# Two attention layers and an expert layer on one core: the batch loop turned by half, the next batch's projections between this batch's last pair and its outputs

## What is computed

```python
# layer 1: self-attention over x, 16 heads of 32
attn = softmax(inner @ outer.T / sqrt(32)) * aperture[..., :, None] * expression[..., None, :]
attn = attn / (attn.sum(-1) + 1e-8);  converged = attn @ v
x1 = layernorm(x + rotate_and_scale(converged) @ Wout)
# layer 2: attention of x1 over ctx, with a mask of 1024 x 1024 for each batch, 16 heads of 32
x2 = layernorm(x1 + softmax(mask(q @ k.T / sqrt(32))) @ v @ Wo + bo)
# layer 3: routed expert attention over x2
```

## Time and profile before

| | us |
|---|---|
| three runs | 4908.39, 4911.23 (median), 4921.20 |
| the profiled execution | 4916.44 |
| its span, from the first to the last instruction | 4914.7 |
| TensorE busy | 4307.2 (88%) |
| VectorE busy | 2653.4 (54%) |
| ScalarE busy | 1568.2 (32%) |
| GpSimd busy | 902.7 (18%) |
| layer 1: first exp of batch 0, last pv of batch 3 | 136.7, 1784.7 |
| layer 2: first exp of batch 0, last pv of batch 3 | 1986.5, 3785.7 |
| last transpose of layer 2 begins | 3834.2 |

### The profile page before, as it was taken

How to read it: one execution, slowest core, us unless ns; L and a number is a source line. 1 busy time by engine, 2 the same in 40 slices (tenths; PEclk the granted TensorE clock), 3 DMA queues, 4 the chain that set the end, 5 groups by cost and what they waited for, 6 DMA issues and landing times. The chain is left out here.

```text
span 4914.7 us, 64052 instructions
## 1 busy us (share of the span) xinstructions
PE 4307.2 (88%) x22296; PEld 2467.3 (50%) x22296; DVE 2653.4 (54%) x3552; ACT 1568.2 (32%) x2813; POOL 902.7 (18%) x616
## 2 busy tenths in 40 slices
PE   5997899789879976999799979997999599989897
PEld 4443643454364434443544354435443376768686
DVE  3563465256345633664466445644664675757584
ACT  1453155225514531343134313431344202020302
POOL 3213311322132223102210221023101100000000
PEclk9999899899989997999899989998999799999898
DMA  3221322222122215210521052105210400010100
GB/s 84 67 65 50 80 47 61 69 65 46 46 83 67 53 37 159 61 40 27 168 61 40 27 168 61 40 27 163 65 40 18 140 18 35 18 35 7 46 1 18
DMA packets 120770, 294.79 MB, mean 60 GB/s; under 512 B 18352, under 2 KB 20272, under 8 KB 120432
## 3 DMA queue, kind: packets, MB, share of 16 engines
q1 hardware_dynamic: 93920, 222.20, 17.4%
q10 hardware_dynamic: 26512, 68.16, 4.1%
HBM read 145.87 MB, written 43.25 MB: 38 GB/s over the span
## 5 line engine op out<-in xcount | busy, mean ns | idle before, releaser
L869 ACT ACTIVATE probs<-half 128x512 f32<-128x512 f32 x2048 | 1113.2, 594 | 1176.0 <-PE half L682 679.8
L677 PE MATMUL half<-stack 97*128 97x512 f32 x2048 | 864.9, 487 | 9.9 <-ACT probs L869 5.6
L1044 DVE TENSOR_REDUCE mx<-wide 128x1 f32<-128x1024 f32 x512 | 603.0, 1220 | 443.2 <-PE wide L643 435.2
L1040 DVE CUSTOM_DVE_ANT_0 wide<-wide,mask_q 128x1024 f32<-128x1024 f32 x512 | 620.1, 1246 | 349.0 <-PE wide L643 341.4
L643 PE MATMUL wide<-stack 96*128 96x512 f32 x2048 | 630.5, 424 | 90.4 <-DMA stack<-qk 35.6
L677 PEld LDWEIGHTS half<-stack 97*128 97x128 f32 x2048 | 371.5, 192 | 600.9 <-issue 373.9
L609 PE MATMUL acc<-probs,v 128*32 128x512 f32 x4096 | 551.4, 609 | 2.9 <-ACT u L855 2.9
L587 PE MATMUL half<-stack,w 128*128 128x512 f32 x1536 | 388.6, 415 | 175.8 <-DVEq L953 151.7
L1386 PE MATMUL work_e<-w_in_e,x_e 128*128 128x512 f32 x2304 | 523.5, 389 | 0.0
L643 PEld LDWEIGHTS wide<-stack 96*128 96x128 f32 x2048 | 384.4, 192 | 200.4 <-DVE mx L1040 52.4
L1386 PEld LDWEIGHTS work_e<-w_in_e,x_e 128*128 128x128 f32 x2304 | 432.2, 188 | 89.7
(11 more groups left out here) (228 smaller groups left out, 3943.7 us busy)
## 6 DMA issues: line engine op xcount, KB each, us to landing
stack<-qk SPq DMA_DIRECT2D x384, 256.0 KB, 4.6
stage<-x_t SPq DMA_DIRECT2D x32, 512.0 KB, 3.5
k_raw<-x SPq DMA_DIRECT2D x8, 2048.0 KB, 9.3
x_t<-xts ACTq DMA_DIRECT2D x16, 1024.0 KB, 7.2
x<-k_raw ACTq DMA_DIRECT2D x8, 2048.0 KB, 8.6
mstage<-mask ACTq DMA_DIRECT2D x32, 512.0 KB, 3.6
mstage<-mask_t ACTq DMA_DIRECT2D x32, 512.0 KB, 3.6
over_a<-over_aperture SPq DMA_DIRECT2D x128, 64.0 KB, 2.7
```

The lines of the kernel that those rows point to most:

```text
L677: last = pe.matmul(bank[:, :], stack[0:3 * DH + 1, s, 2 + h, kt * P:(kt + 1) * P], stack[0:3 * DH + 1, s, h, c * CH:(c + 1) * CH], start=T ...
L869: act.activation(probs[:, kt % 2 * 2 + h, c * CH:(c + 1) * CH], bank[:, :], ACT.Exp, scale=SCALE).then_inc(free, 1)
L1040: dve.tensor_tensor_reduce(bank[:, :], bank[:, :], mask_q[:, t, :], 1.0, -3e38, ALU.add, ALU.max, mx[:, p % 2, n:n + 1]).then_inc(free, 1)
L1044: dve.tensor_reduce(mx[:, p % 2, n:n + 1], bank[:, :], AX.X, ALU.max).then_inc(free, 1)
```

## The change

The list of steps is made anew and the batch loop is cut at another place. Instead of four turns there is a section that only prepares batch 0, a loop of three turns, each with the pairs of batch i and then the projections of batch i+1, and a section with the pairs and the end of batch 3:

```diff
-            with pe.Fori(0, B) as i:
+            run(Section(0, None, False, True, lists[0]))
+            with pe.Fori(0, B - 1) as i:
+                run(Section(1, i, True, True, lists[1]))
+            run(Section(2, None, True, False, lists[2]))
```

```diff
+SLOT = (0, 1, 2, 0, 1, 2, 1, 0)
+MAXIMA = ((2, 3, 3, 3, 3, 3, 2, 2),) + ((2,) * 8,) * 4 + ((2, 3, 3, 3, 3, 3, 1, 0), (2, 2, 2, 2, 1, 0, 0, 0), (0,) * 8)
+def pair_steps(masked, nxt):
+    units = lambda p: [("sm", p, h, t) for h in range(2) for t in range(TT)]
+    ahead = [m for p in range(1, 6) for m in units(p)] + units(7)[:7] + units(6) + units(7)[7:]
...
+            if kt == 0 and p in (1, 2, 3, 4, 5):
+                steps.append(("stack", {1: 3, 2: 4, 3: 5, 4: 7, 5: 6}[p]))
...
+            if nxt and kt == 1 and p == 5:
+                steps += [("load", "wv", 0), ("load", "wv", 1), ("split", "wv", 0), ("split", "wv", 1)]
+            if nxt and kt == 0 and p == 6:
+                steps += [("load", "xk", 0), ("load", "xk", 1)]
+                if masked:
+                    steps += [("mload", 0), ("mload", 1)]
+            if nxt and kt == 0 and p == 7:
+                for k in range(KT):
+                    steps.append(("split", "xk", k))
+                    if k < 2:
+                        steps.append(("load", "xk", k + 2))
...
+            if not masked and nxt and p == 7 and kt in (5, 6):
+                steps.append(("EX", kt - 5))
+            if masked and nxt and p == 7:
+                steps += [("mask", kt), ("mload", kt + 2)]
```

```diff
-                    if step in (("Q", KT - 1, NC_ - 1), ("K", KT - 1, NC_ - 1), ("V", TT - 1), ("out", TT - 1)):
-                        pe.drain().then_inc(proj_done, 1)
-                    if kind == "out":
-                        pe.drain().then_inc(out_done, 1)
```

More of the change, by code:

```diff
@@ L31 @@
 I32 = mybir.dt.int32
-def attention_steps(masked):
-    norm_at = {0: (0,), 1: (1,), 2: (2,), 3: (3,)} if masked else {4: (0,)}
[L37 to L58, removed]
+SLOT = (0, 1, 2, 0, 1, 2, 1, 0)
+HALF_KINDS = ("Q", "K", "EX", "AP", "V", "CS", "st", "out", "xt", "xpad")
+WIDE_KINDS = ("sm", "mneg", "sel", "RZ", "wpad")
+CHUNKS = {"xk": KT, "xq": KT, "wv": 2, "wk": 2, "wq": 2, "wo": 2}
+MAXIMA = ((2, 3, 3, 3, 3, 3, 2, 2),) + ((2,) * 8,) * 4 + ((2, 3, 3, 3, 3, 3, 1, 0), (2, 2, 2, 2, 1, 0, 0, 0), (0,) * 8)
+def pair_steps(masked, nxt):
+    units = lambda p: [("sm", p, h, t) for h in range(2) for t in range(TT)]
+    ahead = [m for p in range(1, 6) for m in units(p)] + units(7)[:7] + units(6) + units(7)[7:]
+    norm_at = {0: (0,), 1: (1,), 2: (2,), 3: (3,)} if masked else {4: (0,)}
+    steps = []
     due = []
@@ L65, in attention_steps @@
             due = []
[L67 to L78, removed]
+            rate = MAXIMA[p][kt]
+            for n in range(rate):
+                m = ahead.pop(0)
+                if n == 2:
+                    continue
+                steps.append(m)
+                if m[2:] == (1, TT - 1):
+                    due.append(("mneg", m[1]))
+            late = [m] if rate == 3 else []
+            if not rate and before[0] >= 0:
                 steps.append(("pv", *before, 0))
@@ L81, in attention_steps @@
             steps += misc
-            if p == 0 and kt:
-                maxima(1)
+            for m in late:
+                steps.append(m)
+                if m[2:] == (1, TT - 1):
+                    due.append(("mneg", m[1]))
             if masked and p == 2 and kt == 4:
@@ L91, in attention_steps @@
                 steps += [("norm", p - 1, part) for part in norm_at[kt]]
+            if not masked and kt == 5 and 0 < p < PAIRS - 1:
+                steps.append(("spread", p + 1))
     assert not ahead and not due
[L93 to L106, removed]
-def attention(nc, masked, io):
[L115 to L122, removed]
+    return steps + [("pv", PAIRS - 1, TT - 1, part) for part in range(2)]
@@ new lines, in _, with parts, chunks_ready @@
+            pe.wait_ge(const_in, 16 * CONSTS)
+            def parts(out, hi_l, lo_l, hi_r, lo_r):
+                for k in range(KT):
+                    for n, (a, b) in enumerate(((hi_l, hi_r), (hi_l, lo_r), (lo_l, hi_r))):
+                        last = pe.matmul(out, a(k), b(k), start=(k == 0 and n == 0), stop=(k == KT - 1 and n == 2))
+                return last
+            def chunks_ready(sec, what):
+                done = ("split", what, CHUNKS[what] - 1)
+                if fast(sec.number, what):
+                    pe.wait_ge(fast_split, fast_splits.upto(sec, done))
+                else:
+                    pe.wait_ge(pool_split, pool_splits.upto(sec, done))
@@ L596, in _, with run @@
+            def run(sec):
+                for step in sec.steps:
                     kind = step[0]
-                    if kind == "norm":
-                        continue
                     if kind == "pv":
@@ new lines, in run @@
+            def run(sec):
+                for step in sec.steps:
+                    kind = step[0]
+                    if kind == "split" and fast(sec.number, step[1]):
+                        _, what, k = step
+                        raw = stage[:, loads.at[sec.number]["load", what, k] % 2, :]
+                        hi, lo = chunk_parts(what, k)
+                        dve.wait_ge(hi_ready, fast_splits.upto(sec, step))
+                        alone(dve)
+                        dve.tensor_tensor(lo, raw, hi.bitcast(F32), ALU.subtract)
+                        dve.drain().then_inc(fast_split, 1)
+                    elif kind == "mask":
+                        n = step[1]
```

1188 lines of the change are left out of this document (668 added, 520 removed).

## The result

The changed kernel takes 4918.5 us (median of 20 runs, 4912.3 to 4933.4), the kernel before 4911.0 in the runs beside it (20 runs): ratio 1.0018, 95% interval 1.001 to 1.0026. It is no faster; the forecast was 4840 us with a range to 4905. Its profiled execution has a span of 4916.7 us.

What follows compares the result with a forecast made beforehand. TensorE was busy 88% of the span, so time could come only from where it isn't, as between batches. Terms -98 -57 -51 +24 +18 +24 +33 +24 +8 = -75 took 4916.4 to 4841, stated as 4840; range 4765 to 4905 us.

Steps and rivals of the forecast that it cites:

- the first pairs: First pair of each batch: TensorE's 6.28 us of idling for pair 1's copies goes, among other savings; -51 us in all.
- Between batches, layer 1: From a batch's last product to the next first exp in layer 1: reordered work leaves 121 us per boundary; -98 us.
- Inside the pairs: Within batches: EX in pair 7 +24, pair 6's late copies +18, its late row +24; x splits and mask pieces nothing.
- Start of layer 2: Stretch from layer 2's first load to its first exp: 155 us for 131.6, behind mask pieces, V and second input; +24 us.
- Boundaries of layer 2: Three stretches between batches in layer 2: 150 us each plus loop ends and half clock, 475 against 532; -57 us.
- 60 more: Unknown clock in the filled stretches between batches: if it stays at 0.86, the total is 60 us longer.
- EX: Two units moved into pair 7: 5.5 us of TensorE and 2.5 of ScalarE waiting, three times; +24 us.
- the first exp: Start of layer 1: x loaded and split, gates, V and all units before any exp; first exp at 170 for 136.7, +33.
- the last batch of layer 2: End of layer 2's last batch: nothing covers residual and bo, ct 0 at T+25 for T+9, less 4 for drains; +12.
- late engines: Rival: ScalarE, VectorE and POOL follow one order and end each boundary 8 us later; 4888 us, chance 0.13.
- Mask pieces one by one: Rival: on SP's queue each mask piece costs 5.2 us against 2.72 of a V unit; 124 us more, 4964; chance 0.10.
- Nothing moves: Rival: the chains, not TensorE's order, set the boundary, and the starts eat the rest; 4911 us, chance 0.05.

Runs made afterwards that it cites:

- the doses: Changed kernel with SP starting pair 4's copies only after the fourth key tile's scores of pair 2, and pair 5's after the fifth tile's of pair 3: 5066.2 us.
- the rates alone: Changed kernel with maxima per key tile of pair 5 set to 2,3,3,3,3,1,3,0 instead of 2,3,3,3,3,3,1,0: 4905.2 us.
- The three edits together: Changed kernel with copies counted by head, maxima 2,3,3,3,3,1,3,0 in pair 5, and its mneg at the end of its key tile: 4806.6 us.
- Another order: Changed kernel with wk loaded before the mask pieces at layer 2's start, four pieces before V, four between V units, eight between K units: 4917.9 us.

## Why the prediction was wrong

- **The boundaries of layer 1 and the first pairs** were right in mechanism and size: 100 us for 98, 49 for 51. The waits under "Between batches, layer 1" came as worked out, but for K (0.56 us for 3) and the loop's end (3.9 for 6.5).
- **The step that failed is "Inside the pairs".** It had seen the late copies of pair 6 (2.8 us in layer 1 and 1.8 in layer 2; measured 3.4 and 2.2 to 2.5) and the late row (3 us; measured 1.8 to 2.5 and 1.7), and it priced each at its length. These waits sum to 38 us where 42 was priced, so their sizes were right. Two things were put at nothing. The first is the stretch at the lower clock behind a stall; the doses show it alone, 2.8 us behind one of 2.9 us and 2.2 behind one of 6.2. The prediction allowed 2 us of it to each boundary, from rows 2, and none to the stalls within the pairs. The second is VectorE: the reciprocal of 3.35 us in the earlier trace rows was not set against three maxima a tile in pair 5, 3.5 us of VectorE each in tiles of 5.0, which makes a third stall of 2.2 us, cured by the rates alone for 13 us. Over all pairs 5 and 6 the trace has 55 us more of idle time than before (the 38 among them), 70 us of TensorE's work at the lower clock, worth 35, and 11 us besides, some of it for the maxima that pair 5 has more: 100. The three edits together are worth 112 us, 36 of them at boundaries and starts, where the wait for pair 0's copies had been priced, and 69 in pairs 5 and 6; 32 of the 100 stay, 22 of them in layer 2.
- **Start of layer 2**, +39 for +20. The end of layer 1's last batch was priced at -4 and gave -3; the first exp comes 173 us after the first load where 155 was worked out. Of these 18 us, 9 are there when V ends (59.6 us for 51, behind the mask pieces, V held for 3.7), 13 when Q begins (105.0 for 92), and 5 come behind it, at a clock of 0.59 in the last 37 us. Another order gave 5 us up to K and moving the column sums gave 3; why the rest is longer is not shown.
- **Boundaries of layer 2**, -37 for -57: two of the three windows are 168 and 166 us where at most 163 was to be right, and the granted clock stayed at 0.83, as in the earlier trace rows, not over 0.9. The four steps of column sums cost 10.9 us among the maxima for 9.1, and their place stretched the maxima to 36 us. Moving them gave 17 us over four places in the profiled execution. The second input was priced about rightly (12 to 13 us for 11.6). The prediction's allowance for a clock that stays low, "60 more", doesn't follow from its own terms: 3 x 14% of 121 is 51, and as much in layer 2 makes over 100.
- **EX, the first exp and the last batch of layer 2** differed by 4, 5 and 11 us, all cheaper than priced. The end of that batch, where residual and bo are no longer covered, is as long as before; why was not looked into.
- **The rivals.** Of "late engines" the trace shows nothing in layer 1's boundaries. "Mask pieces one by one" was wrong where it should decide: in the boundaries of layer 2 VectorE holds V units up for 1.7 to 2.1 us each in all; only at layer 2's start do the pieces share in the 9 us. "Nothing moves" gives the right number, 4911, for a wrong reason: the boundaries did shorten, by 136 us. So the measured time agrees with that rival only because a gain and a loss came out alike. The forecast's own test ("pairs longer than 36 and 39 us" make it wrong) is the one that struck.

## What to carry to other kernels

Price a stall of TensorE as its length plus a stretch at half speed behind it, and count the stalls, not only their sum: three of 2.2 to 3.4 us, 8 in all, made a pair of 39 us 11 longer. The addition was 2.1 to 2.8 us behind stalls of 2.9 us and more. Behind those of 2.1 to 2.4 it was 1.4 us in one measured case, and four had no lower clock behind them at all, so it is a range and not a constant. When a change pulls a transfer's buffer free later, look at what waits for all parts of the transfer but needs one: counting the copies by head was a few lines and gave 74 us. And before a step is moved into a steadily filled stretch, write down for each in-order queue what stands behind it there, VectorE's reciprocal as well as SP's copies.

## What was not expected of the hardware

- Behind a stall of 2.90 us in an otherwise full stretch TensorE ran 6.3 us at a granted clock of 0.51. In one of 6.19 us the clock fell after 3.3 us, within the stall, and TensorE was at full speed 4.3 us after it. Already a wait of 2.17 us was followed by eight products in 1.95 us instead of 1.07, while another of 2.17 us had a clock of 1.00 behind it.
- 16 matmul records with 128 columns of weights and one column of data took 3.4 us, 64 with 32 columns 3.0 us, in stretches at 0.55 and 0.59: the time goes with the columns of weights.
- At the loop's end TensorE stands 3.9 to 4.3 us before the first scores, four times in all; ScalarE's 6.96 us don't reach it in full. Behind one of these, from 1028.5 to 1040.4 us, the granted clock was 0.50.
